# Three-pass expert products with weights split for each tile, in a decoder layer with sparse experts

## What is computed

```python
logits = x @ gate_w
scores = softmax(logits)                     # T = 2048 tokens, E = 8 experts
topk_w, topk_idx = top_k(scores, 2)
comb = zeros((T, E)).at[arange(T)[:, None], topk_idx].add(topk_w)
g = silu(einsum('td,edh->teh', x, w_gate)) * einsum('td,edh->teh', x, w_up)   # H = 352
routed = einsum('teh,ehd,te->td', g, w_down, comb)
shared = silu(x @ sw_gate) * (x @ sw_up) @ sw_down                            # 704 wide
x = layernorm(x + routed + shared)
```

## Time and profile before

| | |
|---|---|
| time, median of 3 runs | 1230.07 us (1230.06 to 1230.31) |
| the profiled execution | 1224.76 us, span of its instructions 1222.8 us |
| granted TensorE clock, mean | 0.935 of full speed |
| busy: PE, PEld, DVE, ACT, POOL | 86%, 55%, 46%, 36%, 34% |
| expert stage | from about 835 us to 1190 us |
| chain of waits that ended last | only the final layer norm, 1% |

### The profile page before, as it was taken

The page is one execution under the profiler, slowest core; times in us unless marked ns, Lnnn a source line. Parts: engine busy times, 40 slices in busy tenths (PEclk is TensorE's granted clock), DMA queues, the critical chain, the costliest instruction groups (busy, mean ns, idle before and its releaser), DMA issues. The chain is left out here.

```text
span 1222.8 us, 16822 instructions
## 1 busy us (share of the span) xinstructions
PE 1052.0 (86%) x4874; PEld 669.7 (55%) x4875; DVE 560.2 (46%) x1221; ACT 440.8 (36%) x759; POOL 418.6 (34%) x423
## 2 busy tenths in 40 slices
PE   5999994999999999617999999963899999999960
PEld 4557882434434433206888888861455555655530
DVE  4226436877777775056777777731111111111104
ACT  4333110666766676323433343321112221221114
POOL 2000000444644645443555555411223323332324
PEclk9999996899999999858999999995989999999995
DMA  7444207232442440031111111105883333333327
GB/s 256 171 160 172 103 1 155 52 93 63 103 97 60 101 103 1 17 136 58 53 53 52 53 52 37 44 24 168 255 265 61 60 68 69 61 59 69 69 35 275
DMA packets 80877, 115.67 MB, mean 95 GB/s; under 512 B 15680, under 2 KB 37056, under 8 KB 80832
## 3 DMA queue, kind: packets, MB, share of 16 engines
q1 hardware_dynamic: 66608, 91.22, 25.2%
q0 software_dynamic: 9760, 20.49, 8.9%
q10 hardware_dynamic: 4464, 3.41, 0.9%
HBM read 74.77 MB, written 40.31 MB: 94 GB/s over the span
## 5 line engine op out<-in xcount | busy, mean ns | idle before, releaser
L553 POOL TENSOR_TENSOR pair_sum<-probs 128x2048 f32<-128x2048 f32 x32 | 146.1, 4566 | 163.6 <-ACT probs L692 163.6
L717 DVE TENSOR_REDUCE maxima<-ps_s 128x8 f32<-128x512 f32 x256 | 168.6, 689 | 70.9 <-PE ps_s L585 69.1
L692 ACT ACTIVATE probs<-ps_st 128x512 f32<-128x512 f32 x256 | 146.6, 600 | 92.8 <-PE ps_st L634 89.2
L1526 POOL DMA_INDIRECT x_dram<-e_y,who x39 | 62.1, 1593 | 213.6 <-ACT e_y L1551 209.9
L585 PE MATMUL ps_s<-k,q 96*128 96x512 f32 x256 | 115.2, 458 | 14.5 <-DMA k<-qk_dram 11.5
L634 PE MATMUL ps_st<-q,k 128*128 128x512 f32 x256 | 121.1, 474 | 4.9 <-ACT probs L692 2.5
L1577 DVE COPY e_gT<-e_ps_gT 128x384 f32<-128x384 f32 x39 | 21.8, 558 | 212.5 <-PE e_ps_gT L1616 212.5
L634 PEld LDWEIGHTS ps_st<-q,k 128*128 128x128 f32 x256 | 49.1, 192 | 109.3 <-ACT probs L692 76.6
L1624 PE MATMUL e_ps_y<-w_all,e_gT 128*128 (+1 forms) x234 | 107.0, 593 | 0.8 <-DVE e_gT L1577 0.8
L1608 PE MATMUL e_ps_g<-w_all,xgT 128*128 x312 | 105.2, 482 | 2.1 <-DMA w_all<-in_L_ffn_w_down_dram 1.1
L1287 PE MATMUL ps_gu<-sw_hi,x2T_hi 128*128 128x352 f32 x256 | 88.0, 344 | 12.7 <-DVE x2T_lo L1168 11.3
(11 more groups left out here) (235 smaller groups left out, 1935.4 us busy)
## 6 DMA issues: line engine op xcount, KB each, us to landing
qk_dram<-qk_ctx SPq DMA_DIRECT2D x32, 512.0 KB, 2.9
q<-qk_dram SPq DMA_DIRECT2D x96, 128.0 KB
k<-qk_dram SPq DMA_DIRECT2D x96, 128.0 KB
w_all<-in_L_ffn_w_gate_dram SPq DMA_DIRECT2D x8, 704.0 KB
w_all<-in_L_ffn_w_up_dram SPq DMA_DIRECT2D x8, 704.0 KB
x_tile<-in_x_dram SPq DMA_DIRECT2D x16, 256.0 KB
x_dram<-x SPq DMA_DIRECT2D x16, 256.0 KB
x_dram<-attn SPq DMA_DIRECT2D x16, 256.0 KB
```

The costliest lines, as they stand in the source:

```text
L553: pool.tensor_tensor(pair_sum[:, h], probs[:, 2 * h], probs[:, 2 * h + 1], ALU.add).then_inc(added, 1)
L692: act.activation(probs[:, kc, j, :], ps_st[:, s % 2, :], ACT.Exp, scale=SCALE).then_inc(exp_done, 1)
L717: dve.tensor_reduce(by_tile[:, t, j, 1:9], ps_s[:, x % 2, :].rearrange("p (g n) -> p g n", n=S // 8), axis=AX.X, op=ALU.max).then_inc(s_re ...
L1526: pool.indirect_dma_start(out=x3_dram[:], out_offset=bass.IndirectOffsetOnAxis(ap=who[:, j, 0:1], axis=0), in_=y[:, p, :], in_offset=None, ...
```

## The change

Each product of the routed experts becomes three passes on `fp32r` operands. The weights of the tile's expert are split anew for each tile: ScalarE writes `w_hi` (gate, up, down: one buffer each), VectorE `w_lo` (the same). x and g are split as they leave PSUM, into two buffers each. The down product now runs over all 128 rows of its third chunk, so VectorE clears the 32 spare rows of it at the start. `xg` has four buffers (XG) in place of two, `ps_xT` and `ps_y` two in place of one. A list no longer waits for the gather two tiles before it, only for the list before. Scatters stand four tiles behind their gathers, in place of three. The y store of tile j stands at the head of ScalarE's tile j+2, in place of the end of tile j+1. The loop now has four tiles. `c.bar` and `c.attn` are allocated in an inner scope that ends before the expert stage.

```diff
+GATE, UP, DOWN = range(3)
+def piece_cols(kind):
+    return slice(kind * DC * FH, (kind + 1) * DC * FH if kind < DOWN else WCOLS)
...
+XG = 4
...
         w = m.sb("w_all", [P, E * WCOLS])
+        w_hi = [m.sb(f"we_hi{k}", [P, (DC * FH, DC * FH, FC * D)[k]], F32R) for k in range(3)]
+        w_lo = [m.sb(f"we_lo{k}", [P, (DC * FH, DC * FH, FC * D)[k]], F32R) for k in range(3)]
         who = m.sb("who", [P, NJ, 2], U32)
-        xg = m.sb("xg", [P, 2, D])
-        xT = m.sb("xgT", [P, 2, D])
+        xg = m.sb("xg", [P, XG, D])
+        xT_hi = m.sb("xgT_hi", [P, 2, D], F32R)
+        xT_lo = m.sb("xgT_lo", [P, 2, D], F32R)
         act_g = m.sb("e_act", [P, 2, FH])
         g = m.sb("e_g", [P, 2, FC * P])
-        gT = m.sb("e_gT", [P, 2, FC * P])
+        gT_hi = m.sb("e_gT_hi", [P, 2, FC * P], F32R)
+        gT_lo = m.sb("e_gT_lo", [P, 2, FC * P], F32R)
         y = m.sb("e_y", [P, 2, D])
-        ps_xT = m.ps("e_ps_xT", [P, D])
+        ps_xT = m.ps("e_ps_xT", [P, 2, D])
         ps_g = m.ps("e_ps_g", [P, S])
         ps_u = m.ps("e_ps_u", [P, S])
...
+        ps_gT = m.ps("e_ps_gT", [P, S])
+        ps_y = m.ps("e_ps_y", [P, 2, D])
...
...
-            with eng.Fori(1, (last - first + 1) // 2) as i:
-                one(2 * i + first, 1)
-                one(2 * i + first + 1, 0)
+        kinds = ("gate", "up", "down")
+        def tiles(eng, one):
+            for j in range(3):
+                one(j, j)
+            with eng.Fori(0, (NJ - 7) // XG) as i:
+                for k in range(XG):
+                    one(XG * i + 3 + k, (3 + k) % XG)
+            for j in range(NJ - 4, NJ):
+                one(j, j % XG)
...
+        def expert_base(eng, j):
+            e = eng.value_load(c.expert_of[0:1, bass.ds(j, 1)], min_val=0, max_val=E - 1)
+            eng.wait_ge(s["w_in"], 64 * e + 64)
+            return e * WCOLS
+        def raw(base, kind):
+            cols = piece_cols(kind)
+            return w[:, bass.ds(base + cols.start, cols.stop - cols.start)]
...
-                    need(sp, s[f"x_in{p}"], 16 * ((j - p) // 2) if isinstance(j, int) else 8 * (j - p))
+                    need(sp, s[f"who{p}"], 16 * ((j - p) // 2) if isinstance(j, int) else 8 * (j - p))
...
-                def gather(j, p):
-                    pool.wait_ge(s[f"who{p}"], 16 * ((j - p) // 2) + 16 if isinstance(j, int) else 8 * (j - p) + 16)
-                    need(pool, s["turned"], j - 1)
+                def gather(j):
+                    pool.wait_ge(s[f"who{j % 2}"], 16 * (j // 2) + 16)
+                    need(pool, s["turned"], j - XG + 1)
...
+                    pool.indirect_dma_start(out=xg[:, j % XG, :], out_offset=None, in_=x2_dram[:],
+                                            in_offset=bass.IndirectOffsetOnAxis(ap=who[:, j, 0:1], axis=0)).then_inc(s[f"x_in{j % XG}"], 16)
...
-                for j in range(NJ):
-                    gather(j, j % 2)
-                    if j >= 3:
-                        scatter(j - 3, (j - 3) % 2)
-                for j in range(NJ - 3, NJ):
-                    scatter(j, j % 2)
+                for j in range(NJ + XG):
+                    if j < NJ:
+                        gather(j)
+                    if j >= XG:
+                        scatter(j - XG, j % 2)
...
-                def x_out(j, p):
+                def w_high(base, kind):
+                    act.activation(w_hi[kind][:], raw(base, kind), ACT.Copy).then_inc(s[kinds[kind] + "_hi"], 1)
+                def x_high(j, p):
                     act.wait_ge(s["turned"], j + 1)
-                    act.activation(xT[:, p, :], ps_xT[:], ACT.Copy).then_inc(s["xT_done"], 1)
+                    act.activation(xT_hi[:, p, :], ps_xT[:, p, :], ACT.Copy).then_inc(s["xT_hi_done"], 1)
...
+                def g_high(j, p):
+                    act.wait_ge(s["gT_turned"], j + 1)
+                    act.activation(gT_hi[:, p, :], ps_gT[:, 0:FC * P], ACT.Copy).then_inc(s["gT_hi_done"], 1)
...
-                def one(j, p, first=False, last=False):
-                    if not last:
-                        x_out(j + 1, 1 - p)
+                def down_high(j):
+                    base = expert_base(act, j)
+                    need(act, s["y_done"], j)
+                    w_high(base, DOWN)
+                def hidden_high(j):
+                    base = expert_base(act, j)
+                    need(act, s["g_done"], j)
+                    w_high(base, GATE)
+                    need(act, s["u_done"], j)
+                    w_high(base, UP)
+                def one(j, r):
+                    p = r % 2
+                    if at(j, 2):
+                        y_store(j - 2, p)
+                    if at(j, 1):
+                        down_high(j - 1)
+                    if not is_last(j):
+                        x_high(j + 1, 1 - p)
                     silu(j, p)
-                    if not first:
-                        y_store(j - 1, 1 - p)
-                x_out(0, 0)
-                one(0, 0, first=True)
-                pairs(act, one, 1, NJ - 3)
-                one(NJ - 2, 1)
-                one(NJ - 1, 0, last=True)
+                    if at(j, 1):
+                        g_high(j - 1, 1 - p)
+                    if not is_last(j):
+                        hidden_high(j + 1)
+                act.wait_ge(s["zeroed"], 1)
+                hidden_high(0)
+                x_high(0, 0)
+                tiles(act, one)
+                y_store(NJ - 2, 1)
+                down_high(NJ - 1)
+                g_high(NJ - 1, 0)
                 y_store(NJ - 1, 0)
...
+                dve.memset(w[FCR:P, :].rearrange("p (e n) -> p e n", n=WCOLS)[:, :, WCOLS - D:WCOLS], 0.0).then_inc(s["zeroed"], 1)
+                def w_low(j, kind):
+                    base = expert_base(dve, j)
+                    dve.wait_ge(s[kinds[kind] + "_hi"], j + 1)
+                    dve.tensor_tensor(w_lo[kind][:], raw(base, kind), w_hi[kind][:].bitcast(F32),
+                                      ALU.subtract).then_inc(s[kinds[kind] + "_lo"], 1)
+                def x_low(j, p):
+                    dve.wait_ge(s["xT_hi_done"], j + 1)
+                    dve.tensor_tensor(xT_lo[:, p, :], ps_xT[:, p, :], xT_hi[:, p, :].bitcast(F32), ALU.subtract).then_inc(s["xT_lo_done"], 1)
...
-                def gT_out(j, p):
-                    dve.wait_ge(s["gT_turned"], j + 1)
-                    dve.tensor_copy(gT[:, p, :], ps_gT[:]).then_inc(s["gT_done"], 1)
-                def one(j, p, first=False):
-                    if not first:
-                        gT_out(j - 1, 1 - p)
+                def g_low(j, p):
+                    dve.wait_ge(s["gT_hi_done"], j + 1)
+                    dve.tensor_tensor(gT_lo[:, p, :], ps_gT[:, 0:FC * P], gT_hi[:, p, :].bitcast(F32), ALU.subtract).then_inc(s["gT_lo_done"], 1)
+                def one(j, r):
+                    p = r % 2
+                    w_low(j, UP)
+                    if at(j, 1):
+                        w_low(j - 1, DOWN)
+                        g_low(j - 1, 1 - p)
+                    if not is_last(j):
+                        x_low(j + 1, 1 - p)
                     multiply(j, p)
+                    if not is_last(j):
+                        w_low(j + 1, GATE)
...
-                gT_out(NJ - 1, 0)
+                w_low(0, GATE)
+                x_low(0, 0)
+                tiles(dve, one)
+                w_low(NJ - 1, DOWN)
+                g_low(NJ - 1, 0)
...
+                def x_turn(j, r):
+                    pe.wait_ge(s[f"x_in{r}"], arrived(j, r))
+                    need(pe, s["xT_lo_done"], j - 1)
                     for q in range(DC):
-                        last = pe.transpose(ps_xT[:, q * P:(q + 1) * P], xg[:, p, q * P:(q + 1) * P], c.ident[:])
+                        last = pe.transpose(ps_xT[:, r % 2, q * P:(q + 1) * P], xg[:, r, q * P:(q + 1) * P], c.ident[:])
...
-                def hidden(j, p, base, up):
-                    if not up:
-                        pe.wait_ge(s["xT_done"], j + 1)
-                    need(pe, s["g_ready"] if up else s["silu_done"], j)
-                    for q in range(DC):
-                        last = pe.matmul((ps_u if up else ps_g)[:, 0:FH], xT[:, p, q * P:(q + 1) * P],
-                                         w[:, bass.ds(base + (up * DC + q) * FH, FH)], start=(q == 0), stop=(q == DC - 1))
-                    last.then_inc(s["u_done"] if up else s["g_done"], 1)
+                def passes(out, stationary, moving, chunks):
+                    for q in range(chunks):
+                        for k, (a, z) in enumerate(((0, 0), (0, 1), (1, 0))):
+                            last = pe.matmul(out, stationary[a](q), moving[z](q), start=(q == 0 and k == 0),
+                                             stop=(q == chunks - 1 and k == 2))
+                    return last
+                def hidden(j, p, kind):
+                    out = ps_u if kind == UP else ps_g
+                    if kind == GATE:
```

(44 more changed lines are left out.)

37 lines of the change are left out of this document (12 added, 25 removed).

## The result

| | before | after |
|---|---|---|
| median of runs, us | 1230.07 (1228.45 to 1230.31) | 1208.68 (1206.93 to 1211.88) |
| the profiled execution, its span, us | 1224.76, 1222.8 | 1209.28, 1207.5 |
| ratio, 95% interval | | 0.983 (0.9815 to 0.9845) |

The change is faster by 21.4 us where 28 were forecast: 1208.7 against 1202, within the range. The two profiled executions lie only 15.5 us apart, because that of before was 5.3 us under its median. What follows accounts for the 15.5; the rest of the 21.4 is read from the medians alone.

The account below looks back on a forecast made before the run. From tile 8 on TensorE's own instructions were taken to bound the kernel, before that the memory. Savings of 26.7 + 4 - 2.4 = 28.3 us from the median 1230.07 gave 1202 us, range 1189 to 1226.

Parts of the forecast that it names:

- Term 1: TensorE's work for a tile of the expert stage after the change: 6.98 us, bounds 6.78 to 7.57.
- rival A: TensorE alone binds the expert stage, waits pass and turns cost nothing more: 6.78 us a tile, 1190 us; chance 0.12.
- Term 2: Splits beside TensorE's work, per tile: ScalarE 6.42 us, VectorE 6.88, both barely below 6.98; 0.1 charged for a register load.
- Term 3: Waits from single-buffered weight halves: down ring 6.95 us a tile, 0.1 added; 7.2 a tile, 26.7 us saved over 29 steps.
- Term 4: Early tiles, gathered rows in four buffers: tile 8's y near 937.5, not 942.49; 4 us saved, bounds 0 and 9.
- rival D: Early tiles 3 to 7 run partly at half clock, tile 8 up to 10 us later: 1216 us; chance 0.06.
- Term 5: End of the expert stage: last y store 6.4 us after the one before, not 3.98; 2.4 us more.
- B: Queues of ScalarE and VectorE bind, loads and handovers add some 0.6 us: 7.8 a tile, 1219 us; chance 0.15.
- C: VectorE stands still during GpSimd's scatter and gather: 9.45 us a tile, slower at 1267 us; chance 0.11.

Follow-up runs that it names:

- two swaps: Changed kernel, with ScalarE copying down weights' high half before the y store and VectorE making the next gate weights' low half before the multiply: 1188.29 us.

## Why the prediction was right, and where its sizes were off

**The direction and the mechanism.** Tiles became shorter because TensorE has less to do, the splits fit beside it, and waits between engines cost something on top: all seen. But it is the ring, and no longer TensorE, that sets the pace. ScalarE's wait before y fell from 5.00 to between 0.85 and 1.42 us, VectorE is at 85%, and its main wait is for the down weights' high half (38.4 of the 40.5 us ahead of that subtraction).

**Where luck helped.** The terms as the traces have them give 20.7 - 2.2 - 4.6 + 1.3 = 15.2 us, against the forecast's 28.3: 13 less. The medians lie 21.4 apart, 6 us of it in no term, since the profiled execution of before was 5.3 us faster than its others. And 7.2 us a tile came from two errors that partly cancel: TensorE taken 0.2 too long, and the waits on top 0.4 too short.

**Term 1** said 6.98 us (bounds 6.78 to 7.57); without splits it is 6.74. The 0.1 for each turn was not there; rival A's 6.78 was TensorE's true size.

**Term 2** was sound: VectorE's 6.88 is 85.4% of 7.40, 6.32; ScalarE's 6.42 is 5.96 (overlapping operations count once there).

**Term 3 is the step that failed in size, and it had the wrong ring.** It traced the down weights from the up products through the next multiply and closed that ring over two tiles at 6.95 us. The ring that binds closes over one tile: down products, y store, high half, low half, g's low half, down products. With the prediction's own figures 2.11 + 0.69 + 1.48 + 1.76 + 0.53 = 6.57; going from each of the five steps to the next adds 0.9 (7.46 less 6.57): 0.48 between the products' 2.11 and the y store, 0.18 ahead of the high half, 0.23 behind it, the rest small. The prediction charged 0.2 in all. So 7.40 instead of 7.2, and 20.7 us instead of 26.7.

**Term 4 failed at the pace of the loads.** It let tile 8 come 4 to 5 us earlier thanks to four buffers, at 937.5; in the trace it came 2.2 later, and no profile with these lists and weights has it before 938.9. Against the one profile of before (942.49) the sign itself lies within their spread. "That pace is the memory's and stays" was the step: the loads took 10.69 us instead of the 10.06 read from the trace of before (the variants show 9.81 to 10.80), so that list 9 landed at about 924.2, when its gather went, and not at 917.6. From there the working holds: rows some 5 us later, at 929.33, and y of tile 8 two tiles behind that. A second thing binds at the same place: tile 8's own rows took 7.2 us to land beside the weights, not the 4.2 of one row, and the pass that follows, partly at half clock, ends at 929.33 too. The traces do not separate the two. The run with two buffers says that four bring nothing. "Moving the scatters a tile back costs nothing" was true and missed the point: not moving them costs 0.2 us a tile, 6 us, since issues have grown and tiles have shrunk. The clock at 0.50 after a pause, rival D's mechanism, is there (900 to 904, 923 to 925); its cost was not measured apart. By "wrong if tile 8's y comes later than 942" this term was wrong.

**Term 5** said 2.4 us more at the end; it is 4.6. ScalarE and VectorE, then TensorE:

```profile
1160.19 1.48 ACT L1576 ACTIVATE we_hi<-w_all 128x1536 fp32r x1
```

```profile
1161.90 1.76 DVE L1638 TENSOR_TENSOR we_lo<-w_all,we_hi 128x1536 fp32r<-128x1536 f32 x1 [4.46 <-ACT we_hi L1576]
```

```profile
1164.18 0.79 PE L1686 MATMUL e_ps_y<-we_hi,e_gT_hi 128*128 128x512 f32 x1 [4.48 <-DVE e_gT_lo L1652]
1164.77 0.63 PE L1686 MATMUL e_ps_y<-we_lo,e_gT_hi 128*128 128x512 f32 x1
```

The chain is the predicted one but for g's low half, 0.55 us between the weights' low half and the products, which the sum left out. The four operations that it did count come to 6.04 us. And after 4.48 us of rest TensorE runs at 0.50 of the clock from 1164 to 1167, with products about 0.43 us apart instead of 0.234, 3.84 us to the y store instead of 2.59: 1.25 us. The other 0.8 are handovers: 6.04 + 0.55 + 1.25 + 0.77 = 8.61.

**The rivals.** A (TensorE alone) is what two swaps make of the kernel. B (the queues of ScalarE and VectorE) is refuted by the same run: with VectorE at 93% a tile still takes 6.82 us, where it takes 6.76 without the splits. C (VectorE and GpSimd exclude each other) is half true: GpSimd's issues grow, VectorE's subtractions do not, and GpSimd at 52% has room. The Trainium skill ("SBUF — State Buffer", section "SBUF: two separate sides") describes this side of it in a box: while VectorE runs an operation in a two-port mode, GpSimd cannot write the descriptors of a transfer that it issues. By that a gather waits for VectorE and not VectorE for a gather. The runs agree on the side that waits, but for subtractions with two inputs in SBUF, which the box does not name: 0.98 against 1.64 us. That the lock itself is the cause was not separated from others.

**The medians.** They differ by 21.4 us and the traces by 15.5. Which part of the kernel before was faster in its profiled execution than in its others is open; a spread of some 6 us in the early tiles, as the variants show, would do, but no second trace of it shows this.

**Not tested.** The two buffers of ps_xT and ps_y and the list that no longer waits for a gather were never undone on their own.
